# On-chip transfers in place of selection matmuls and copies in an attention and mixture-of-experts kernel

## The reference

```python
# attention: 16 heads of 8, segments of 128 tokens in a fixed (snake) order, every second key
qkv = layernorm(x) @ w_qkv.T
qh, kh, vh = (part[:, :, perm] for part in split(qkv))
kd, vd = kh[..., ::2, :], vh[..., ::2, :]            # per segment of 128: 64 keys
attn = softmax(einsum('bhsqd,bhskd->bhsqk', qh * 8 ** -0.5, kd))
o = einsum('bhsqk,bhskd->bhsqd', attn, vd) @ w_out.T
x = x + layernorm(o)
# experts, on xf = layernorm(x)
probs = softmax(xf @ router_w)                       # 8 experts, the best 2 count
routed = sum over the best 2 of prob * (silu(xf @ w1[e]) @ w2[e])
shared = sigmoid(xf @ gate_w) * ((silu(gate) * up) @ down)
x = x + layernorm(routed + shared)
```

## Time and profile before

| | us |
|---|---|
| median of 3 runs | 159.79 (159.53 to 160.01) |
| the profiled execution | 159.69 |
| its span, first to last instruction | 157.6 |

### The profile page before, as it was taken

One profiled execution on the slowest core, in us unless ns is written; L12 is line 12 of the kernel. 1 busy time (PEld: TensorE's weight loads), 2 busy tenths in 40 slices (PEclk: granted clock), 3 DMA queues, 4 the chain that ended last, 5 costly groups with the idle time before them and its releaser, 6 DMA issues.

```text
span 157.6 us, 3642 instructions
## 1 busy us (share of the span) xinstructions
PE 144.3 (92%) x1188; PEld 125.1 (79%) x1188; DVE 132.3 (84%) x499; ACT 113.8 (72%) x269; POOL 47.0 (30%) x47
## 2 busy tenths in 40 slices
PE   6799999999997999999999999999989999699900
PEld 5488887887795789888889889999979999599900
DVE  6979998887899989897986697999999449975992
ACT  3797979877985799846999896476983769177603
POOL 6642102000061040400520005894330994020221
PEclk9999999999999999999999999999999999999996
DMA  5999900000000000000000000000002000200202
GB/s 149 284 283 299 183 13 0 0 4 0 0 4 0 0 4 0 4 2 2 0 4 0 0 4 0 0 2 4 2 0 67 4 2 0 67 0 4 67 0 67
DMA packets 10625, 6.01 MB, mean 38 GB/s; under 512 B 752, under 2 KB 10608, under 8 KB 10608
## 3 DMA queue, kind: packets, MB, share of 16 engines
q1 hardware_dynamic: 10192, 5.58, 13.0%
q10 hardware_dynamic: 416, 0.21, 0.4%
HBM read 3.69 MB, written 1.05 MB: 30 GB/s over the span
## 4 chain that ended last, share of the span: by engine, by line
PE 77%; DVE 9%; ACT 5%; issue 3%; DMA 2%; POOLq 1%; ACTq 1%; POOL 0%; DVEq 0%
PE bank L625 18%; PE bank L502 8%; PE bank L366 6%; PE bank L479 5%; PE bank L519 5%; PE bank L367 5%; PE bank L368 5%; PE bank L552 3%; PE bank L532 3%; DMA cst<-in_consts 2%; PE bank L451 2%; DVE X L1477 2%; PE bank L459 2%; PE bank L452 2%; PE bank L423 2%
## 5 line engine op out<-in xcount | busy, mean ns | idle before, releaser
L299 POOL TENSOR_TENSOR RS<-VE,nhalf 128x4 f32<-128x4 f32 x14 | 14.1, 1011 | 65.1 <-DVE VE L1255 65.1
L1477 DVE SCALAR_TENSOR_TENSOR X<-bank,CW,X 128x128 f32<-128x128 f32 x80 | 22.5, 343 | 7.8 <-PE bank L625 7.5
L625 PEld LDWEIGHTS bank<-w2n,Pr 128*128 128x128 f32 x192 | 25.0, 191 | 2.0
L625 PE MATMUL bank<-w2n,Pr 128*128 128x128 f32 x192 | 25.1, 275 | 0.0
L1350 DVE TENSOR_REDUCE negm<-bank 128x8 f32<-128x512 f32 x32 | 21.4, 685 | 3.0 <-PE bank L479 2.6
L1045 ACT ACTIVATE Pr<-bank 128x512 f32<-128x512 f32 x27 | 16.3, 605 | 8.9 <-PE bank L368 8.7
L980 ACT ACTIVATE Pr<-bank 128x512 f32<-128x512 f32 x32 | 18.7, 597 | 4.0 <-PE bank L502 3.6
L502 PE MATMUL bank<-Qs,Kb 128*128 128x128 f32 x128 | 18.8, 274 | 0.0
L502 PEld LDWEIGHTS bank<-Qs,Kb 128*128 128x128 f32 x128 | 16.8, 191 | 2.1 <-issue 1.2
L319 POOL TENSOR_TENSOR Tm<-Tm 128x512 f32<-128x512 f32 x7 | 9.0, 1285 | 21.9 <-ACT Tm L1060 21.9
L479 PE MATMUL bank<-Kb,Qs 96*128 96x256 f32 x64 | 14.2, 314 | 1.2 <-DVE negm L1350 0.8
(11 more groups left out here) (158 smaller groups left out, 351.0 us busy)
## 6 DMA issues: line engine op xcount, KB each, us to landing
...
Kb<-kone SPq DMA_DIRECT2D x8, 128.0 KB, 4.4
...
out<-XN SPq DMA_DIRECT2D x2, 128.0 KB, 1.8
...
```

Of the source, the lines that this page charges most:

```text
L299: nc.gpsimd.tensor_tensor(RS[:, k, b], VE[:, k, b], nhalf[:], ALU.pow).then_inc(pw[k], 1)
L625: i = mm(ps[output_bank(n, s)][:, s * P:(s + 1) * P], lhs[:, s * P:(s + 1) * P], w, start=True, stop=True)
L1477: V.scalar_tensor_tensor(out=acc[:, b, t], in0=ps[output_bank(n)][:, t * P:(t + 1) * P], scalar=CW[:, b, t, k:k + 1], in1=acc[:, b, t], op ...
```

## The change

**Rearranging by DMA.** The host permutes the query and key rows of w_qkv so that group g's 32 rows are every fourth row; the four heads with place h in their groups then lie in rows 32h to 32h+31. `q_place` then copies the whole of `qch` or `qcl`, 128 rows of 2 KB, into 32 partitions of `Qs` by 4 groups, three times (high, high, low); `k_place(b, j)` copies, per part j and head h, 32 rows of `kch` or `kcl` into 8 partitions of `Kb` in pieces of 64 columns (256 bytes), so 12 transfers of 32 KB per batch. SP issues them between its loads, but for batch 1's queries (`q_place_1`), which ScalarE issues. The loads of w1, w_out, X, w2 and down move behind them. Batch 0's keys still go by matmul, copy and product, the latter now over 128 rows with the ones of rows 96 to 127 from masks. `Kb` has three buffers. `select_q_0`, `select_q`, `select_k`, `q_rows`, `q_rows_0`, `k_rows` and `k_blocks` are gone (scores_q of batches 1 to 3 waits for `q_in` and `k_in` instead), as are the eight `kone` transfers.

**GpSimd's new work.** `key_fill(u, s)` writes buffers 1 and 2 of `Kb` whole from the constants, which leaves zeros outside a head's rows and ones in rows 96 to 127: eight operations of 128x1024. `add_rows` is moved from VectorE to GpSimd as a product and a sum of 128x512.

**Router.** The weights lie side by side as (low, high, zero), so two matmuls of 20 columns replace three of 10; VectorE adds the pairs as it copies. **End.** VectorE subtracts the mean ahead of the power (`cen`), ScalarE adds the shift to TR beforehand (`last_shift`), and after the power one product and sum per tile (`last_out`) writes the output. **Orders.** The lists of all four engines are new, with fewer warm-up matmuls.

```diff
+        Kb = sb("Kb", [P, KBUF, G, NT, HG, KEYS], F32R)
+        TR = XP
+            def q_place_0(h):
+                for j in range(PARTS):
+                    sp.wait_ge(S["ql" if j == 2 else "qh"], h + 1)
+                    part = (qcl if j == 2 else qch)[:, TH * h:TH * (h + 1)]
+                    sp.dma_start(Qs[32 * j:32 * j + 32, 0, :, TH * h:TH * (h + 1)].bitcast(F32),
+                                 part.bitcast(F32)).then_inc(q_in0[h], 16)
+            def q_place(b):
+                if b >= 2:
+                    sp.wait_ge(S["s2"], 8 * (b - 1))
+                for j in range(PARTS):
+                    sp.wait_ge(S["ql" if j == 2 else "qh"], b + 2)
+                    sp.dma_start(Qs[32 * j:32 * j + 32, b % 2].bitcast(F32),
+                                 (qcl if j == 2 else qch)[:].bitcast(F32)).then_inc(q_in[b], 16)
+            def k_place(b, j):
+                if b >= KBUF:
+                    sp.wait_ge(S["s2"], 8 * (b - KBUF + 1))
+                else:
+                    sp.wait_ge(S["kf"], NT * b)
+                sp.wait_ge(S["kl" if j == 1 else "kh"], b + 2)
+                for h in range(HG):
+                    sp.dma_start(Kb[32 * j + HD * h:32 * j + HD * (h + 1), b % KBUF, :, :, h].bitcast(F32),
+                                 (kcl if j == 1 else kch)[32 * h:32 * (h + 1)].bitcast(F32)).then_inc(k_in[b], 16)
+            q_place_0(0)
+            q_place_0(1)
+            for j in (0, 2, 1):
+                k_place(1, j)
             sp.dma_start(w1n[:], w1.rearrange("e d f -> d e f")).then_inc(S["ld_w1"], 16)
+            sp.dma_start(woT[:], w_outT).then_inc(S["ld_wout"], 16)
+            for j in (0, 2, 1):
+                k_place(2, j)
+            sp.dma_start(X[:, 0], x_v[0]).then_inc(ld_x[0], 16)
+            q_place(2)
+            for b in range(1, B):
+                sp.dma_start(X[:, b], x_v[b]).then_inc(ld_x[b], 16)
-            sp.dma_start(woT[:], w_outT).then_inc(S["ld_wout"], 16)
-            for b in range(B):
-                sp.dma_start(X[:, b], x_v[b]).then_inc(ld_x[b], 16)
-            sp.wait_ge(S["kones"], 1)
-            for u in range(2):
-                for s in range(NT):
-                    sp.dma_start(Kb[MROW:P, u, :, s].bitcast(F32), kone[MROW:P].bitcast(F32)).then_inc(kdma[u], 16)
+            for j in (0, 2, 1):
+                k_place(3, j)
+            q_place(3)
...
+            def key_fill(u, s):
+                if u == 1 and s == 0:
+                    pool.wait_ge(S["ld_cst"], 16)
+                    pool.wait_ge(S["vones"], 4)
+                nc.gpsimd.tensor_copy(Kb[:, u, :, s], cst[:, C_ONE:C_ONE + G * HG].rearrange(
+                    "p (g h) -> p g h", g=G).unsqueeze(3).to_broadcast([P, G, HG, KEYS])).then_inc(S["kf"], 1)
...
+            def add_rows(b):
+                pool.wait_ge(pw[1], b + 1)
+                pool.wait_ge(S["xn"], NT * (b + 1))
+                nc.gpsimd.tensor_tensor(TR[:, b], Y[:], RS[:, 1, b].unsqueeze(2).to_broadcast([P, NT, D]),
+                                        ALU.mult).then_inc(S["yr"], 1)
+                pool.wait_ge(S["yr"], b + 1)
+                pool.wait_ge(ld_x[b], 16)
+                nc.gpsimd.tensor_tensor(TR[:, b], TR[:, b], X[:, b], ALU.add).then_inc(S["tr"], NT)
...
-            def select_k(b, halves=(0, 1)):
...
-                        pe.wait_ge(S["qs_a"], 2 * (s // HT) + half + 1)
+                        pe.wait_ge(q_in0[s // HT], 16 * PARTS)
-                    elif half == 0:
-                        pe.wait_ge(S["qs_a"], 3 * b + 3)
-                        pe.wait_ge(S["kb_d"], HG * (b + 2))
-                        pe.wait_ge(S["qs_a"], 3 * b + 4)
-                        pe.wait_ge(S["qs_d"], b)
+                        pe.wait_ge(q_in[b], 16 * PARTS)
+                        pe.wait_ge(k_in[b], 16 * PARTS * HG)
...
-                    o = x3_bank(b)[:, s * RC:(s + 1) * RC]
-                    mm(o, xh, rwh[:], start=True, stop=False)
-                    mm(o, xh, rwl[:], start=False, stop=False)
-                    i = mm(o, xl, rwh[:], start=False, stop=True)
+                    o = x3_bank(b)[:, s * 2 * RC:(s + 1) * 2 * RC]
+                    mm(o, xh, rws[:, 0:2], start=True, stop=False)
+                    i = mm(o, xl, rws[:, 1:3], start=False, stop=True)
...
             def q_high(b):
 
                 act.wait_ge(S["qc"], b + 2)
-                act.wait_ge(S["qs_ps"], G * b)
+                for done in q_in0 if b == 1 else (q_in[b - 1],):
+                    act.wait_ge(done, 16 * PARTS)
             def k_high(b):
-                act.wait_ge(S["ks_ps"], 2 * b)
+                if b == 1:
+                    act.wait_ge(S["ks_ps"], 2)
+                else:
+                    act.wait_ge(k_in[b - 1], 16 * PARTS * HG)
...
+            def last_out(h):
+
+                b = B - 1
+                dve.wait_ge(pw[3], B + h)
+                if h == 0:
+                    dve.wait_ge(S["trm"], NT)
+                    dve.wait_ge(stored[b - 2], 16)
+                for t in range(HT * h, HT * (h + 1)):
+                    dve.wait_ge(S["cen"], t + 1)
+                    V.scalar_tensor_tensor(out=FO[:, b % 2, t], in0=acc[:, b, t], scalar=RS[:, 3, b, t:t + 1],
+                                           in1=TR[:, b, t], op0=ALU.mult, op1=ALU.add).then_inc(S["fo"], 1)
 
...
+    part = np.arange(D).reshape(G, D // G).T.reshape(-1)
+    laid["L0_attn_w_qkv"] = laid["L0_attn_w_qkv"][np.concatenate([part, D + part, 2 * D + np.arange(D)])]
```

590 lines of the change are left out of this document (255 added, 335 removed), and 4 rows, old and new, of the table names.

## The result

| | before | after |
|---|---|---|
| median, us | 159.66 (159.50 to 160.01) | 177.56 (176.58 to 181.48) |
| ratio after to before | | 1.110 (1.106 to 1.113) |
| profiled execution, its span | 159.69, 157.6 | 176.58, 174.8 |
| granted clock, mean | 0.991 | 0.893 |

Slower by 11%, where 3.7% faster was forecast. One of the four executions after, the one of 181.48, was in a state in which the cores of a die get a lower clock and all kernels take some per cent longer; such executions are left out from here on, which gives 176.8 us for the changed kernel. TensorE has less work, as planned, and a smaller share of the chain; what came in is waiting for DMA and SP's queue. The page of the changed kernel: 40 slices of 4.4 us, with the granted clock and the busy share of the DMA engines in tenths, then the chain's shares and the costliest of its lines.

What follows compares the result with a forecast made beforehand. From 25.6 us on TensorE's own work was taken to bound the kernel, before that a chain through all engines. Seven stretches summed to a span of 151.7, plus 2.1 around it: 153.8 us, range 148.8 to 158.8.

Steps and rivals of the forecast that it cites:

- What bounds the kernel, and what leaves TensorE: From 25.6 us on TensorE's own work bounds; removed selection matmuls save 2.9 us in each of two stretches, router 0.45 to 0.9.
- The transfers: On SP's queue, a batch's keys take 6.3 us of issues, queries 1.6, plus 1.8 to land; costed at nothing.
- The cover given for the keys: Spare time for batches' key transfers on SP: gone if twelve take over 7.3 us.
- the sum: Seven stretches, 26.9, 12.9, 14.8, 15.3, 23.1, 50.5 and 8.2 us: span 151.7, plus 2.1 around it, 153.8.
- A cover of 1 to 3 us: Each set of key and query transfers lands 1 to 3 us before TensorE wants it.
- The second rival: Key transfers in 256-byte pieces are slow, at 14 us per batch the time is 160.8 us; chance 0.13.
- The fills: At the start, GpSimd's key fills hold VectorE's NM: first XN 2.1 us late, another 1.5 later; first stretch 26.9 us.
- The residual: Moved to GpSimd, two operations of 1.29 us; batch 3's delays VectorE, costing 0.3 us (0 to 1.5).
- The 0.8 us that TensorE lost to it in 40 to 58: TensorE's loss to GpSimd's w1l, still behind a power, was kept in the forecast time.
- The end: After the last matmul group, the shorter last chain takes 0.3 us less (0 to 0.6): 8.2 us for 8.5.
- The third rival: GpSimd's residual and fills block VectorE in 40 to 98 us while TensorE waits for maxima: 159.0 us; chance 0.09.

Runs made afterwards that it cites:

- the two kernels with the parts built in: The kernel before with the new router and shorter last chain: 159.04 us; with its ScalarE additions later 158.11; with the residual on GpSimd too 157.74.
- the fillers' run: The changed kernel with matmuls on zeros, 14 ahead of batch 1's first query scores and 9 ahead of batch 3's: 172.25 us.
- all mends: The changed kernel with later fills, batch 0's key products in a row, ten filler matmuls, batch 3's queries issued sooner and last_shift behind the loop: 176.4 us.

## Why the prediction was wrong

- **What bounds the kernel, and what leaves TensorE: right.** With the query bytes away the stretches came out at 12.6 and 14.6 (12.9 and 14.8 forecast), the next at 16.0 (15.3). The router's matmuls were 0.11 apart.
- **The transfers: the step that failed.** "Its queries 3 more, 1.6 us" and "queries landed at 54.2" sized a query set at its issues plus 1.8 us, the landing of 128 KB spread over all partitions. It is 768 KB into 96 partitions, 32 at a time: 8.0 us alone. The row nearest to it was the 4.4 us of Kb<-kone, 128 KB into 32 partitions, in the same group; I had put that down to load. The cover given for the keys, 7.3 us, was also passed (9.0). The profile names them in none of TensorE's long waits, but they had a part in both: batch 1's copies took 13.3 us beside them and 8.4 beside a quarter of them, and batch 3's queries were issued 2.7 us late behind them. And the sum let each set run as if nothing else were in flight, for which it gave no row.
- **The missing term: the clock.** The sum takes 2.4 GHz for granted. A wait was priced at its length; it costs its length and the half clock behind it, 13.3 us for 4.1. A cover of 1 to 3 us over four batches is no cover at such a price.
- **The second rival: right in sign, wrong in cause.** It priced the key pieces of 256 bytes. Their size is innocent (3.3 to 3.4 us for 256 KB in any pieces). Late keys did come, as it had them: ScalarE's k_high waited 5.7 us for their landing; but what made them late was the length of the issues and what was in flight beside them. It had no clock either: 160.8 for 176.8. The Trainium skill (DMA: Bandwidth & Descriptors, Why small descriptors are slow (HBM only)) had that about the pieces right; whoever dropped the rival by it dropped the outcome too.
- **The fills: mechanism right, size partly.** XN was 1.6 us late for 2.1; but fills hold the key products too (1.9 us at 19.9), which the step left out, and the first stretch is 29.9 without query bytes, 3.0 above the forecast. In that run the clock is near half for some 8 us of this stretch (0.52, 0.63, 0.58 and 0.57 in the windows of 2 us at 10, 12, 20 and 22 us), where before it was 1.00 throughout. What these windows lack to 1.00 is 3.4 us together, so the clock alone could be all of the 3.0. Or it is VectorE's new order: no run tells the two apart.
- **The residual: mis-sized.** 0.3 us for batch 3 is 0.8, inside its bounds of 0 to 1.5; a gain of 0.87 in the third stretch was not foreseen. "The 0.8 us that TensorE lost to it in 40 to 58 stays in my sum" was wrong: the residual, in its new place, kept NM away from w1l.
- **The end: right in kind, smaller, and paid for.** 149.1, where the prediction cut the kernel before, is not the end of its last matmul group:

```profile
147.97 2.01 PE L625 MATMUL bank<-w2n,Pr 128*128 128x128 f32 x16
```

It ends at 149.98, so the end was 7.6 us and not 8.5, and the 0.9 us belong to the stretch ahead. Cut alike, the end is now 7.53 us, 0.1 less where 0.3 was forecast (7.40 in the two kernels with the parts built in), and the stretch ahead took 52.15 us where the forecast comes to 51.4. That 0.75 is about the 0.8 us that the additions cost ahead of the last silu. I counted their use and not their place.
- The third rival (the lock eats the gain in 40 to 98 us) did not come: nothing in the third stretch, with a residual in it, waits for it. That this stretch is as forecast (14.68 for 14.8) is in part luck: the 0.8 us for w1l that the sum kept in it is gone, and about as much came in from elsewhere; no run shows from where.

Open: what ended the half clock. After a pause of 5.6 us it lasted 20 us, after one of 4.1 also 20, after one of 3.9 (the changed kernel, at 74.5) 6 to 7, some 2.5 of it still inside the pause, after one of 2.5 (the fillers' run) 3.4, after one of 2.3 some 17, after one of 1.3 (all mends) 13, with TensorE busy behind nearly all of them. The length of the pause does not tell it, and no run here tells what does.
